# A windowed-attention kernel on one core: smaller first loads, v masked by ScalarE in the first strip, a wait moved in the loop, and fifteen matmuls ahead of the first strip

## Chip, cores and metric

One NeuronCore of a Trainium2 chip runs the kernel in one launch. The metric is the device time in microseconds (us); it is the median of three runs. All data are float32.

## What is computed

The input is an image batch of 4 x 128 channels x 96 x 96. It is normalised by groups, goes through ReLU linear attention in windows of 4 x 4 pixels, once on the projected pixels and once on their 5 x 5 average pools, then through a projection with batch normalisation, and is added to the input.

```python
def _gn(v, G=32, eps=1e-05):
    ...
    return ((g - m) / jnp.sqrt(s + eps)).reshape(v.shape)      # over 4 channels and all pixels

def _L0_conv_ref(x, qkv_w, proj_w, bn_gamma, bn_beta, bn_mean, bn_var):
    # x is cut into windows of 4 x 4 pixels
    qkv = jnp.einsum('nchw,oc->nohw', xw, qkv_w)
    pooled = _avg_pool5(qkv)
    msq = jnp.concatenate([qkv, pooled], axis=1)               # 16 heads of each, 8 numbers
    q, k = relu(msq[..., :8]), relu(msq[..., 8:16])
    v = jnp.pad(msq[..., 16:], ..., constant_values=1.0)       # a ninth column of ones
    kv = jnp.einsum('ngld,nglm->ngdm', k, v)
    out = jnp.einsum('ngld,ngdm->nglm', q, kv)
    out = out[..., :-1] / (out[..., -1:] + 1e-15)
    ...
    y = jnp.einsum('nchw,oc->nohw', out, proj_w)
    return y * inv[None, :, None, None] + (bn_beta - bn_mean * inv)[None, :, None, None]

x = x + _L0_conv_ref(_gn(x), ...)
```

## The kernel before

The 96 rows of each of the four images are cut into strips of four rows: 24 strips of an image, 96 in all, each with 384 pixels (24 windows) in the free dimension and the channels on the partitions. All of x stays on chip, in `x_all`. The order of work is written out by hand for each engine; semaphores tie the engines together, each with a count that goes up by one a strip.

**Head.** SyncE (SP) issues six loads of four strips each (L216) and then the constants and weights (L219), which raise `loaded_w`. VectorE takes the statistics of each strip as its load lands (L453), forms the group mean and variance (L461 to L488, with one square root by ScalarE, L407), normalises strip 0 (L517, signal `xn_ready`) and pools it (L509, signal `xp_ready`). GpSimd does the same for strip 1 (L286, L292, L264) and for all later strips.

**One strip.** TensorE multiplies the normalised strip by the weights of k and v (`conv_kv`, L659: three matmuls; `conv_kv_pooled`, L668: two). ScalarE writes k with ReLU (`relu_k`, L344, signal `km_f`) and copies v (`copy_v`, L355, signal `v_copied`). The windows of a tile must be kept apart in the product of k and v. For the full part this is done by four DMAs (`spread_v`, L234, signal `vm_f`) that copy every fourth row of `v_full` into its own copy in `vm_full`, which is zero elsewhere; for the pooled part by six ScalarE passes with a scale of 0 or a weight per partition (`masked_v_pooled`, L366, signal `vm_p`), between the second and the third of which `copy_y_pooled` (L403, signal `y_copied`) copies the pooled result of the strip before. `kv_products` and `kv_products_pooled` (L687) form k·v, VectorE masks it by heads (`own_heads`, L561, signals `kvc_f`, `kvc_p`), `out_products` and `out_products_pooled` (L703) multiply with q, VectorE divides (L592 to L596), TensorE transposes (L778) and projects (`project`, L787 and L789, signals `y_f`, `y_p`). VectorE adds the full part to x (L567, signal `added_f`), GpSimd the pooled part (`residual_pooled`, L264), and SP stores the strip.

**Order on TensorE.** Each pass through `step` handles the convolution of strip s + 1, transposes and projection of strip s - 1, output products of strip s, and the products of k and v of strip s + 1. Steps 1 to 94 are a loop of two steps a round. A PSUM bank serves several purposes, which is what some of the waits are for: banks 2 and 3 take the convolution and later the pooled output products, banks 0 and 1 the projection and later the products of k and v. Ahead of the pooled output products stands a wait for `added_f` and `y_copied` with a no-op (L756 to L758).

**Between the head and the loop** the batch normalisation is folded into the projection: VectorE computes its factors after ScalarE's second square root and scales `proj_sb` (L629 to L637, signal `proj_scaled`), TensorE transposes it (L811), VectorE copies it out (L644, signal `projT_ready`) and fills the ones columns of `vm_pool` (L641, signal `ones_set`).

## Time and profile before

| | |
|---|---|
| runs | 887.57, 884.42, 886.83 us; median 886.83 |
| profiled execution | 886.18 us, of which its span 884.3 us |
| TensorE (PE) busy | 848.4 us, 96% of the span |
| VectorE (DVE) busy | 699.9 us, 79% |
| GpSimd (POOL) busy | 658.9 us, 75% |
| ScalarE (ACT) busy | 480.9 us, 54% |
| DMA, mean over the span | 68 GB/s |

The span runs from the first instruction to the last. The profile gives times in microseconds from its start. PE is the stream of matmuls, PEld the loading of their weights, SPq the DMA queue's issues. One float32 matmul shows as two records. "Idle before" is the time that an engine stood still ahead of a row, and what released it; "issue" means that the profile shows nothing that it waited for.

### The profile page before, as it was taken

The numbers are of one execution on the slowest core, as the hardware profiler recorded it, in microseconds if no ns is written. First come the engines' busy times: TensorE is split into PE (matmuls) and PEld (weight loads), VectorE is DVE, ScalarE is ACT, GpSimd is POOL, SyncE is SP. The second block draws the span as 40 slices with busy tenths as digits, with TensorE's granted clock in tenths as the row PEclk, the third lists the DMA queues.
The fourth block names the chain that finished last, engine by engine and source line by source line (L and its number), as shares of the span: only waits on it lengthen the run. The fifth ranks groups of instructions, "written<-read, shape, count | busy, mean of one in ns | idle before, by whom it ended". The sixth has DMA issues, their size and how long they took to land.

```text
span 884.3 us, 63772 instructions
## 1 busy us (share of the span) xinstructions
PE 848.4 (96%) x28322; PEld 693.0 (78%) x28322; DVE 699.9 (79%) x1252; ACT 480.9 (54%) x1349; POOL 658.9 (75%) x1624
## 2 busy tenths in 40 slices
PE   0789999999999999999999999999999999999997
PEld 0568888888888888888888888888888888888885
DVE  7758888887778888888777888888777777777776
ACT  0346565646465655555555556565656564646563
POOL 2558787878787878777878777787878787878781
PEclk9999999999999999999999999999999999999999
DMA  6122322111123323111113232211111111111111
GB/s 236 40 77 81 103 84 82 49 47 48 47 69 97 91 94 98 51 48 47 49 50 99 86 98 88 82 51 48 48 50 46 49 48 47 48 47 48 47 49 47
DMA packets 39081, 60.06 MB, mean 68 GB/s; under 512 B 8560, under 2 KB 33648, under 8 KB 39024
## 3 DMA queue, kind: packets, MB, share of 16 engines
q1 hardware_dynamic: 39024, 59.52, 20.0%
q14 instruction: 48, 0.39, 0.1%
q8 instruction: 9, 0.15, 0.1%
HBM read 19.38 MB, written 18.87 MB: 43 GB/s over the span
## 4 chain that ended last, share of the span: by engine, by line
PE 94%; DVE 3%; issue 1%; DMA 1%; SPq 0%; ACT 0%; DVEq 0%
PE ps L703 24%; PE ps L687 17%; PE ps L659 14%; PE ps L668 9%; PE ps L675 9%; PE ps L787 7%; PE ps L778 6%; PE ps L789 4%; PE ps L676 4%; DVE stats L453 1%; DMA x_all<-x 0%; DVE kvc_full L561 0%; DVE kvc_pool L561 0%; DMA vm_full<-v_full 0%; DVE kvc_full L509 0%
## 5 line engine op out<-in xcount | busy, mean ns | idle before, releaser
L366 ACT ACTIVATE vm_pool<-ps,cst 128x256 f32<-128x256 f32 x576 | 230.1, 480 | 0.0
L376 ACT ACTIVATE q_full<-ps 128x384 f32<-128x384 f32 x96 | 47.2, 491 | 281.0 <-PE ps L675 281.0
L561 DVE TENSOR_TENSOR kvc_full<-ps,cst 128x864 f32<-128x864 f32 x192 | 193.2, 1048 | 4.7 <-PE ps L687 4.7
L561 DVE TENSOR_TENSOR kvc_pool<-ps,cst 128x864 f32<-128x864 f32 x192 | 193.2, 1048 | 0.5 <-PE ps L687 0.5
L286 POOL TENSOR_TENSOR xd<-x_all,mean_t 128x384 f32<-128x384 f32 x95 | 78.6, 827 | 154.3 <-PE ps L676 137.8
L659 PE MATMUL ps<-wkv_sb,xn 128*128 128x256 f32 x576 | 141.4, 382 | 23.1 <-DVE xn L517 23.1
L264 POOL TENSOR_TENSOR x_all<-y_pool,x_all 128x96 f32<-128x96 f32 x380 | 148.9, 424 | 12.7 <-DVE x_all L567 7.2
L659 PEld LDWEIGHTS ps<-wkv_sb,xn 128*128 128x128 f32 x576 | 109.4, 191 | 33.2 <-issue 23.0
L703 PEld LDWEIGHTS ps<-kvc_full,q_full 64*32 64x32 f32 x9216 | 108.3, 105 | 26.0 <-issue 26.0
L292 POOL TENSOR_TENSOR xn<-xd,rstd_t 128x96 f32<-128x96 f32 x380 | 121.8, 367 | 8.1 <-DVE xn L517 0.7
L703 PE MATMUL ps<-kvc_full,q_full 64*32 64x72 f32 x9216 | 125.0, 230 | 0.6 <-DVE kvc_pool L561 0.6
L703 PE MATMUL ps<-kvc_pool,q_pool 64*32 64x72 f32 x9216 | 116.1, 231 | 2.3 <-issue 2.2
L567 DVE SCALAR_TENSOR_TENSOR x_all<-ps,shift,x_all 128x384 f32<-128x384 f32 x96 | 59.3, 618 | 62.3 <-PE ps L787 57.7
L703 PEld LDWEIGHTS ps<-kvc_pool,q_pool 64*32 64x32 f32 x9216 | 101.8, 105 | 3.1 <-issue 3.0
L668 PE MATMUL ps<-wkv_sb,xp 128*128 128x256 f32 x384 | 99.7, 382 | 0.7 <-ACT q_pool L384 0.6
L687 PE MATMUL ps<-vm_full,k_full 64*32 64x144 f32 x4608 | 95.4, 288 | 2.3 <-issue 1.5
L687 PE MATMUL ps<-vm_pool,k_pool 64*32 64x216 f32 x3072 | 94.9, 345 | 1.9 <-issue 1.9
L264 POOL TENSOR_TENSOR hs<-ht,xn 128x96 f32<-128x96 f32 x190 | 84.0, 442 | 14.9
L355 ACT ACTIVATE v_full<-ps 128x384 f32<-128x384 f32 x96 | 47.3, 492 | 86.1 <-PE ps L659 86.0
L592 DVE TENSOR_SCALAR den_full<-ps 128x48 f32<-128x48 f32 x96 | 20.0, 208 | 90.1 <-PE ps L703 89.7
L675 PE MATMUL ps<-xn,wq_sb 128*128 128x384 f32 x192 | 87.6, 538 | 0.0
L787 PE MATMUL ps<-o_sb,projT 128*128 128x384 f32 x192 | 78.5, 491 | 0.0
(74 smaller groups left out, 1316.2 us busy)
## 6 DMA issues: line engine op xcount, KB each, us to landing
vm_full<-v_full SPq DMA_DIRECT2D x384, 54.0 KB, 1.9
out<-x_all SPq DMA_DIRECT2D x96, 192.0 KB, 1.9
x_all<-x SPq DMA_DIRECT2D x36, 384.0 KB, 3.4
x_all<-x SPq DMA_DIRECT2D x6, 768.0 KB, 7.9
cst<-consts SPq DMA_DIRECT2D x1, 170.0 KB, 11.0
wkv_sb<-wkv SPq DMA_DIRECT2D x1, 128.0 KB, 10.8
o_sb<-proj SPq DMA_DIRECT2D x1, 128.0 KB, 10.1
wq_sb<-wq SPq DMA_DIRECT2D x1, 64.0 KB, 10.6
```

The lines of the kernel that those rows point to most:

```text
L264: return pool.tensor_tensor(o, a, b, ALU.add)
L286: link(pool.tensor_tensor(xd[:], x_all[:, s * SP:(s + 1) * SP], mean, ALU.subtract), 1)
L292: last = pool.tensor_tensor(xr[:, r], rows[:, r], rstd, ALU.mult)
L366: last = act.activation(heads[:, e, :, :, 0:D], src, ACT.Copy, scale=col(C_VP + e))
L561: last = dve.tensor_tensor(kvc[:, g], src.to_broadcast(shape), own, ALU.mult)
L567: dve.scalar_tensor_tensor(xs, ps[:, Y_F, 0:SP], shift[:], xs, ALU.add, ALU.add).then_inc(added_f, 1)
L659: last = pe.matmul(ps[:, bank, at:at + 2 * P], xn[:, p, t * P:(t + 1) * P], wkv_sb[:], start=True, stop=True)
L668: last = pe.matmul(ps[:, KV_P, t * 2 * P:(t + 1) * 2 * P], xp[:, p, t * P:(t + 1) * P], wkv_sb[:], start=True, stop=True)
L675: pe.matmul(ps[:, Q_F, 0:SP], wq_sb[:], xn[:, p], start=True, stop=True).then_inc(q_f, 1)
L687: last = pe.matmul(ps[Q4 * i:Q4 * (i + 1), bank + r, t * n:(t + 1) * n], k[rows, t, Q4 * i:Q4 * (i + 1)], vm[rows, :, t, i * KC:(i + 1) * KC],
L703: last = pe.matmul(ps[Q4 * c:Q4 * (c + 1), bank + g, t * n:(t + 1) * n], blocks[rows, 4 * t + c, Q4 * e:Q4 * (e + 1)], kvc[rows, r, w], st ...
L787: pe.matmul(ps[:, Y_F, 0:SP], projT[:, 0:P], o_sb[:, 0:SP], start=True, stop=True).then_inc(y_f, 1)
```

## The change

1. The first image is loaded in nine pieces of 1, 1, 2, 4, 4, 4, 4, 2 and 2 strips in place of six of four.
2. `vm_full` of strip 0 is no longer filled by a copy and four DMAs but by four ScalarE passes straight from PSUM with a scale of 0 or 1 per partition (`masked_v_first`, signal `vm_first`); the constants have four new columns for it. The second square root stands after these passes.
3. GpSimd writes the ones columns of both masked copies once the weights are there; VectorE wrote those of `vm_pool` before.
4. TensorE turns the projection after `kv_products(0)`, in another bank, in place of ahead of the convolution of strip 1.
5. TensorE runs fifteen matmuls of 256 columns on ones before its first real matmul, as soon as weights and memsets are done.
6. In the loop the wait ahead of the pooled output products is gone. A wait for `km_f` stands ahead of the pooled projection, and a wait for `y_copied` ahead of `kv_products`. On ScalarE `copy_y_pooled` comes one pass later and waits for `added_f` too.

```diff
+        pieces = [1, 1, 2] + [4] * (FOURS - 2) + [2, 2]
...
         GS = 16
+        WARM_UP = 15
...
-            for i in range(FOURS):
-                sp.dma_start(x_all[:, 4 * i * SP:4 * (i + 1) * SP],
-                             x_v[:, 0, 4 * i * SP:4 * (i + 1) * SP]).then_inc(loaded_first[i], 16)
+            at = 0
+            for i, n in enumerate(pieces):
+                sp.dma_start(x_all[:, at:at + n * SP], x_v[:, 0, at:at + n * SP]).then_inc(loaded_first[i], 16)
+                at += n * SP
...
-            spread_v(0)
...
             pool.wait_ge(pads_zero, 5)
+            pool.wait_ge(loaded_w, 16 * 5)
+            for vm, n, first_col in ((vm_full, EF, C_VF), (vm_pool, EP, C_TP)):
+                for e in range(n):
+                    ones = vm[:, e].rearrange("p t (h c) -> p t h c", c=HC)[:, :, :, D]
+                    last = pool.tensor_copy(ones, col(first_col + e).unsqueeze(2).to_broadcast(list(ones.shape)))
+            last.then_inc(ones_set, 1)
...
+            def masked_v_first():
+
+                act.wait_ge(conv_f, 1)
+                act.wait_ge(ones_set, 1)
+                heads = vm_full[:].rearrange("p e t (h c) -> p e t h c", c=HC)
+                src = kv_tiles(KV_F, TF)[:, :, P:].rearrange("p t (h m) -> p t h m", m=D)
+                for e in range(EF):
+                    last = act.activation(heads[:, e, :, :, 0:D], src, ACT.Copy, scale=col(C_VF + e))
+                last.then_inc(vm_first, 1)
...
-                    if between is not None and e == 1:
+                    if between is not None and e == 2:
                         copy_y_pooled(between)
...
             def copy_y_pooled(s):
+
                 act.wait_ge(y_p, s + 1)
+                act.wait_ge(added_f, s + 1)
...
+            pe.wait_ge(pads_zero, 5)
+            ones = v_full[:].rearrange("p t c -> p (t c)")
+            for i in range(WARM_UP):
+                pe.matmul(ps[:, KV_P, 0:2 * P], ones[:, 0:P], ones[:, 0:2 * P], start=True, stop=True)
...
-                pe.wait_ge(vm_f, 16 * EF * (s + 1))
+                if is_first(s):
+                    pe.wait_ge(vm_first, 1)
+                else:
+                    pe.wait_ge(vm_f, 16 * EF * s)
+
+                wait(pe, y_copied, s - 1)
                 pe.nop(nofuse=True)
...
-                else:
-
-                    pe.wait_ge(added_f, s)
-                    pe.wait_ge(y_copied, s)
                     pe.nop(nofuse=True)
...
                 pe.wait_ge(o_p, s + 1)
+                if out_next:
+                    pe.wait_ge(km_f, s + 3)
                 pe.matmul(ps[:, Y_P, 0:SPP], projT[:, P:2 * P], o_sb[:, SP:],
```

TensorE at the start of the program, before: the convolution of strip 0 stands first, and the projection (`cst,o_sb`) is turned ahead of the convolution of strip 1.

```order
L659 MATMUL ps<-wkv_sb,xn 128x256 [waits xn_ready,loaded_w]
L659 MATMUL ps<-wkv_sb,xn 128x256 x2
L668 MATMUL ps<-wkv_sb,xp 128x256 [waits xp_ready]
L668 MATMUL ps<-wkv_sb,xp 128x256
L811 MATMUL ps<-cst,o_sb 128x128 [waits proj_scaled]
L811 MATMUL ps<-cst,o_sb 128x128
L659 MATMUL ps<-wkv_sb,xn 128x256 [waits xn_ready,km_f,v_copied]
L659 MATMUL ps<-wkv_sb,xn 128x256 x2
L687 MATMUL ps<-vm_full,k_full 32x144 [waits vm_f,km_f,projT_ready,ones_set]
```

The same place of the changed kernel, line numbers its own:

```order
L680 MATMUL ps<-v_full 128x256 [waits pads_zero,loaded_w]
L680 MATMUL ps<-v_full 128x256 x14
L688 MATMUL ps<-wkv_sb,xn 128x256 [waits xn_ready]
L688 MATMUL ps<-wkv_sb,xn 128x256 x2
L697 MATMUL ps<-wkv_sb,xp 128x256 [waits xp_ready]
L697 MATMUL ps<-wkv_sb,xp 128x256
L688 MATMUL ps<-wkv_sb,xn 128x256 [waits xn_ready,km_f,vm_first]
L688 MATMUL ps<-wkv_sb,xn 128x256 x2
L716 MATMUL ps<-vm_full,k_full 32x144 [waits km_f,vm_first]
L716 MATMUL ps<-vm_full,k_full 32x144 x23
L847 MATMUL ps<-cst,o_sb 128x128 [waits proj_scaled]
L847 MATMUL ps<-cst,o_sb 128x128
```

Fifteen matmuls stand ahead, and the two transposes have moved behind the products of strip 0, which no longer wait for the projection.

TensorE in the loop, from the projection to the products of the next strip, before:

```order
L787 MATMUL ps<-o_sb,projT 128x384 [waits kvc_p,o_f]
L789 MATMUL ps<-o_sb,projT 128x216 [waits o_p]
L703 MATMUL ps<-kvc_full,q_full 32x72 x48
L703 MATMUL ps<-kvc_pool,q_pool 32x72 [waits added_f,y_copied]
L703 MATMUL ps<-kvc_pool,q_pool 32x72 x47
L712 REGISTER_ALU
L687 MATMUL ps<-vm_full,k_full 32x144 [waits vm_f]
```

And in the changed kernel:

```order
L816 MATMUL ps<-o_sb,projT 128x384 [waits kvc_p,o_f]
L820 MATMUL ps<-o_sb,projT 128x216 [waits km_f,o_p]
L732 MATMUL ps<-kvc_full,q_full 32x72 x48
L732 MATMUL ps<-kvc_pool,q_pool 32x72 x48
L744 REGISTER_ALU
L716 MATMUL ps<-vm_full,k_full 32x144 [waits vm_f,y_copied]
```

The wait in the middle of the 96 output products is gone, and the one for the pooled copy stands at the products of k and v.

## Rows read from the trace of the kernel before

**Rows 1.** Windows: stretch, its length, busy time by engine (instructions), TensorE's clock, DMA.
```profile
61.45:65.20 3.75, 3.75 (x118) 2.86 (x119) 2.39 (x5) 0.00 (x0) 0.00 (x0) 0.54 0.16 58
78.78:87.53 8.75, 8.75 (x296) 7.18 (x295) 7.50 (x14) 4.97 (x15) 6.86 (x18) 1.00 0.31 93
...
400.00:600.00 200.00, 199.96 (x6780) 164.17 (x6778) 163.18 (x287) 114.09 (x322) 158.06 (x391) 1.00 0.22 71
```

**Rows 2.** The line that loads the first image: duration in ns, starts, landing.
```profile
L216 SPq DMA_DIRECT2D x_all<-x x6: 386/438/715, 0.7 to 3.4; - x6
...
DMA to landing us min/median/max: 4.4/7.9/11.2
```

**Rows 3.** Timeline of the head: start, length, engine, line, operation, idle time before.
```profile
5.20 11.29 DVE L453 BATCH_NORM_STATS2 stats<-x_all 128x6 f32<-128x384 f32 x24 [4.31 <-DMA x_all<-x]
...
5.87 0.48 SPq L219 DMA_DIRECT2D o_sb<-proj  x1
...
21.45 0.90 POOL L286 TENSOR_TENSOR xd<-x_all,mean_t 128x384 f32<-128x384 f32 x1 [16.46 <-DVE rstd_t L488]
...
23.08 2.90 PE L659 MATMUL ps<-wkv_sb,xn 128*128 128x256 f32 x6 [23.08 <-DVE xn L517]
...
26.13 1.83 PE L668 MATMUL ps<-wkv_sb,xp 128*128 128x256 f32 x4 [0.15 <-DVE xp L509]
26.29 0.20 ACT L407 ACTIVATE std<-var 128x1 f32<-128x1 f32 x1 [5.96 <-DVE var L629]
...
26.91 0.35 POOL L264 TENSOR_TENSOR vt<-hs 128x72 f32<-128x72 f32 x1
...
28.28 2.29 ACT L366 ACTIVATE vm_pool<-ps,cst 128x256 f32<-128x256 f32 x6
...
28.33 0.44 PE L811 MATMUL ps<-cst,o_sb 128*128 128x128 f32 x2 [0.37 <-DVE o_sb L637]
...
28.88 0.41 DVE L644 COPY projT<-ps 128x256 f32<-128x256 f32 x1
...
30.85 0.98 PE L687 MATMUL ps<-vm_full,k_full 64*32 64x144 f32 x48 [0.78 <-DMA vm_full<-v_full]
...
31.91 2.02 DVE L561 TENSOR_TENSOR kvc_full<-ps,cst 128x864 f32<-128x864 f32 x2 [2.63 <-PE ps L687]
```

**Rows 4.** The page's DMA issues: KB each, us from issue to landing.
```profile
o_sb<-proj SPq DMA_DIRECT2D x1, 128.0 KB, 10.1
```

**Rows 5.** The chain of waits in order of time: a convolution at full clock.
```profile
43.05 1.29 PE ps L659 x6
```

**Rows 6.** Timeline of TensorE around its last stall in new code.
```profile
61.45 0.79 PE L703 MATMUL ps<-kvc_pool,q_pool 64*32 64x72 f32 x37 [2.19 <-issue]
...
65.06 0.93 PE L675 MATMUL ps<-xn,wq_sb 128*128 128x384 f32 x2
```

**Rows 7.** Timeline of a strip in the loop, all engines.
```profile
76.97 2.38 SPq L234 DMA_DIRECT2D vm_full<-v_full  x4
...
77.44 0.51 ACT L344 ACTIVATE k_full<-ps 128x384 f32<-128x384 f32 x1
...
78.32 0.53 PE L789 MATMUL ps<-o_sb,projT 128*128 128x216 f32 x2
...
78.78 1.29 PE L703 MATMUL ps<-kvc_full,q_full 64*32 64x72 f32 x96
78.88 0.35 ACT L403 ACTIVATE y_pool<-ps 128x216 f32<-128x216 f32 x1
...
79.85 1.20 PE L703 MATMUL ps<-kvc_pool,q_pool 64*32 64x72 f32 x96
...
80.97 0.98 PE L687 MATMUL ps<-vm_full,k_full 64*32 64x144 f32 x48
```

**Rows 8.** The line that normalises strip 0: duration in ns, least, median and most.
```profile
L517 DVE TENSOR_SCALAR xn<-x_all,mean_t,rstd_t x4: 359/373/882, 21.3 to 22.6; 128x96 f32<-128x96 f32 x4
```

**Rows 9.** The page's costliest groups: busy us, mean ns, idle us before.
```profile
L703 PE MATMUL ps<-kvc_pool,q_pool 64*32 64x72 f32 x9216 | 116.1, 231 | 2.3 <-issue 2.2
```

More of the change, by code:

```diff
@@ L37 @@
 C_TP = C_VP + EP
-C_PACK = C_TP + EP
+C_VF = C_TP + EP
+C_PACK = C_VF + EF
 N_CONST = C_PACK + P
@@ L57, in constants @@
     c[:, C_TP:C_TP + EP] = own_p * times
+    c[:, C_VF:C_VF + EF] = p[:, None] % EF == np.arange(EF)[None]
     pads = p % Q4 >= WP * PXP
@@ L149, in build @@
         loaded_w = sem("loaded_w")
-        loaded_first = [sem(f"loaded_first{i}") for i in range(FOURS)]
+        pieces = [1, 1, 2] + [4] * (FOURS - 2) + [2, 2]
+        assert sum(pieces) == SPB
+        loaded_first = [sem(f"loaded_first{i}") for i in range(len(pieces))]
         loaded_later = sem("loaded_later")
@@ L158, in build @@
         ones_set = sem("ones_set")
+        vm_first = sem("vm_first")
         mv_zero = sem("mv_zero")
@@ L227, in spread_v @@
             def spread_v(s):
-                sp.wait_ge(v_copied, s + 1)
+                sp.wait_ge(v_copied, s)
                 wait(sp, kv_f, s)
@@ L353, in copy_v @@
                 act.wait_ge(conv_f, s + 1)
-                wait(act, vm_f, 16 * EF * s)
+                wait(act, vm_f, 16 * EF * (s - 1))
                 act.activation(v_full[:].rearrange("p t (h c) -> p t h c", c=HC)[:, :, :, 0:D],
@@ L409, in _ @@
             square_root(0)
-            square_root(1)
             act.wait_ge(loaded_w, 16 * 5)
@@ L430, in step @@
                     square_root(b + 1)
-            copy_v(0)
+            masked_v_first()
             relu_k(0)
+            square_root(1)
             relu_k_pooled(0)
@@ L532, in _ @@
             dve.wait_ge(mv_zero, 1)
-            for i in range(FOURS):
+            at = 0
+            for i, n in enumerate(pieces):
                 dve.wait_ge(loaded_first[i], 16)
-                for at in range(4 * i, 4 * i + 4):
+                for at in range(at, at + n):
                     last = gather_strip(0, at)
-                last.then_inc(gathered, 1)
+                    if at % 4 == 3:
+                        last.then_inc(gathered, 1)
+                at += 1
             dve.wait_ge(gathered, FOURS)
@@ L637, in _ @@
             dve.tensor_scalar(proj_sb, proj_sb, bn_inv[:], None, ALU.mult).then_inc(proj_scaled, 1)
-            for e in range(EP):
-                ones = vm_pool[:, e].rearrange("p t (h c) -> p t h c", c=HC)[:, :, :, D]
-                last = dve.tensor_copy(ones, col(C_TP + e).unsqueeze(2).to_broadcast(list(ones.shape)))
-            last.then_inc(ones_set, 1)
             dve.wait_ge(proj_turned, 1)
-            dve.tensor_copy(projT[:], ps[:, TRF, 0:2 * P]).then_inc(projT_ready, 1)
+            dve.tensor_copy(projT[:], ps[:, Q_F, 0:2 * P]).then_inc(projT_ready, 1)
             over_strips(step)
@@ L746, in out_products_pooled @@
             def out_products_pooled(s):
-                if is_first(s):
-                    pe.wait_ge(km_f, s + 2)
-                    pe.nop(nofuse=True)
-                elif is_last(s):
-                    pe.wait_ge(kvc_p, s + 1)
-                    pe.nop(nofuse=True)
-                else:
-                    pe.wait_ge(added_f, s)
-                    pe.wait_ge(y_copied, s)
+                if is_first(s) or is_last(s):
+                    if is_first(s):
+                        pe.wait_ge(km_f, s + 2)
+                    else:
+                        pe.wait_ge(kvc_p, s + 1)
                     pe.nop(nofuse=True)
@@ L807, in _ @@
             conv_kv_pooled(0, 0)
+            pe.wait_ge(vm_first, 1)
+            pe.wait_ge(km_f, 1)
+            conv_kv(1, 1)
+            kv_products(0)
             pe.wait_ge(proj_scaled, 1)
             for z in range(2):
-                last = pe.transpose(ps[:, TRF, z * P:(z + 1) * P], proj_sb[:, z * P:(z + 1) * P], col(C_IDENT, P))
+                last = pe.transpose(ps[:, Q_F, z * P:(z + 1) * P], proj_sb[:, z * P:(z + 1) * P], col(C_IDENT, P))
             last.then_inc(proj_turned, 1)
-            pe.wait_ge(v_copied, 1)
-            pe.wait_ge(km_f, 1)
-            conv_kv(1, 1)
+            kv_products_pooled(0)
             pe.wait_ge(projT_ready, 1)
-            pe.wait_ge(ones_set, 1)
-            kv_products(0)
-            kv_products_pooled(0)
             conv_q(0, 0)
```

## The prediction

> **What bounds the kernel now.** I read the busy time by stretch first. From 200 us to the end the matmul engine is busy all the time at the full 2.4 GHz: 199.96 of 200 us in [rows 1]. The reader is to see there that in the loop nothing but TensorE's own instructions counts; VectorE, ScalarE and GpSimd have room. So an edit pays in two places only: before TensorE is saturated (the head, 0 to some 66 us) and in what TensorE itself issues in each of the 94 looped strips. A strip takes 8.75 us: the second window of [rows 1] runs from one start of a group of matmuls, 78.78, to its next, 87.53.
>
> The head I read as a timeline. Six pieces of four strips each are loaded; the first lands 4.4 us after its issue at 0.7, the last 11.2 us after its issue at 3.4, that is at 5.1 and 14.6 [rows 2], or 0.475 us of transfer per strip. VectorE's 24 statistics fill 5.20 to 16.49, 0.47 us each. So the loads and VectorE run at the same pace, and the chain from there (group mean and variance, first normalised strip) gives TensorE its first matmul at 23.08. Between 23.08 and 28.3 matmuls take about twice their later time. Then a ring follows: v is copied, four transfers spread it, the products start at 30.85 when these have landed, and VectorE's masking starts at 31.91 [rows 3].
>
> **The first pieces (1, 1, 2, 4, 4, 4, 4, 2, 2).** VectorE can begin earlier, but strips 5 to 8 still come as one piece, which lands at 5.1 + 4 x 0.475 = 7.0, and before the change VectorE got to strip 5 at 5.20 + 4 x 0.47 = 7.08. What was gained before that is spent waiting. Behind it each piece of four lands just as VectorE is done with the last. Strips 17 to 20 land at 14.6 - 4 x 0.475 = 12.7; eight strips from there end at 12.7 + 8 x 0.47 = 16.46, against 16.49 before. Worth 0.0 us. SP issues three loads more, some 0.44 us each [rows 2], ahead of the weights, but the weights queue behind the 14.6 us of x anyway: the last lands at 5.87 + 10.1 = 15.97 [rows 3, 4]. Bounds: 0.5 better (only the first strips' lead) to 0.5 worse (smaller pieces landing more slowly).
>
> **Fifteen matmuls on ones.** They wait for the weights (taken 16.1) and the memsets, and stand ahead of the first real matmul. At full clock a pair of passes over 256 columns takes 1.29 / 3 = 0.43 us [rows 5], at half clock 0.86. Two stretches show when the clock rose: after the pause before 61.45 TensorE is granted 0.54 of its clock until some 3.6 us later, 65.06 [rows 1, 6]; from 23.08 its matmuls are slow to between 27 and 28.3, 4 to 5.2 us [rows 3]. I take 4: 4.6 matmuls cold, 10.4 warm: 4.0 + 4.5 = 8.5, end at 24.6. Ends: 3.6 gives 24.4; 5.2 gives 25.3; a clock that is up at once 22.6 (then xn at 23.0 decides); one that never rises 29.0. So the ones last longer than the wait that they fill, by 1.6 us, and the first product then takes 1.3 instead of 2.6 to 2.9 [rows 3]: it ends at 24.6 + 1.3 = 25.9, just as before. The gain of the clock is paid for by the overshoot. The pooled product no longer waits for it: xp is there at 26.13, and 1.83 us become 0.9.
>
> **v masked by ScalarE.** Removed are one copy of v and the four transfers that release the products at 30.85. Added are four ScalarE passes of 128 x 384 with a scale. Not in the trace; the pooled form, 128 x 256, costs 2.29 / 6 = 0.38 [rows 3], so between 4 x 0.38 = 1.5 and, by columns, 2.3; I take 1.9. Path: product done 26.0, v masked 27.95, then k (0.5 as in [rows 7]) 28.45, second square root 28.6, product of strip 1 28.5 to 29.8, masked products 1.06 (30.85 to 31.91) to 30.85. Projection: from the end of the square root (26.29 + 0.20) to the transposes took 28.33 - 26.49 = 1.84, so 28.6 + 1.84 = 30.45, hidden by those products. The two transposes (0.44) and the copy of projT (0.41) now stand between the products and VectorE's masking: 31.7, less some 0.2 since they enter while the products drain, 31.5. Before it was 31.91. The pooled v (2.29 from 28.7) is ready at 31.0, under it. So the head gains 0.4 on the path that starts the loop. With the ones ended at 23.0 it would be some 1.6 us more, 2.0 in all.
>
> **GpSimd writes the ones columns.** Ten small copies after the weights, each no dearer than GpSimd's vt row, 0.35 for more columns [rows 3], so at most 3.5 us, done by 19.7, before 21.45 where GpSimd starts. They run beside VectorE's chain. One of its four equal operations on xn took 882 ns instead of 373 [rows 8], and GpSimd's xd ran just then [rows 3]. If all the copies fell on VectorE, xn would come up to 3.5 us later; xn has 1.6 us of cover under the ones, so cost 0, ceiling 1.9. The Trainium skill (SBUF — State Buffer, two separate sides) says that the two engines' shared port is an exclusive lock, against VectorE operations in a two-port mode or with two inputs in SBUF. By that rule only the two-input operations of that chain could be held up, each by no more than a copy, and the cost stays 0. By that rule, too, an operation that meets GpSimd's waits for all of it, which the 882 ns row bears out: it ended with xd.
>
> **The loop.** Three edits, and they are three waits moved. The wait and the no-op ahead of the pooled output products go. Equal groups of 96 passes start at 78.78, 79.85 and (the next) 80.97: 1.07 and 1.12 us, so at most 0.05 us per strip lies there, 4.7 us over 94 [rows 7]. From below: TensorE idled 2.3 us in all ahead of this group [rows 9], 2.19 of them in one stall [rows 6], so 0.1 over 95. I take 1.0 us, 0.01 a strip, nearer the idle row, since idle time is what a wait can give back. Added: the wait for k ahead of the pooled projection. k is written by 77.95, that matmul starts 78.32 [rows 7]: 0.37 of cover. Added: y_copied at the v·k products. The copy ended 79.23 and comes one pass (0.38) later, 79.6; the products start 80.97. Cover 1.35; behind it nothing of ScalarE is late, since its passes are the same ones. GpSimd reads the copy after 81. What is late next if TensorE gets faster is the fourth v transfer: issued by about 78.8, landed 1.9 later, 80.7, needed 80.97: 0.25 of cover, so the loop can give no more than that.
>
> **Sum.** 0.0 - 0.4 - 1.0 = -1.4 us. The profiled execution took 886.18 (span 884.3, some 1.9 around it) and becomes 884.8; it is 0.65 under the median of the runs, 886.83, which becomes 885.4.
>
> **Rivals.**
> The wait in the loop costs all of the 0.05. For it: the two equal groups do differ by that. Against: they differ in operands too, and the idle time is 0.1. Then -4.7 and 0.4 to 2.0 from the head: 881.7 to 880.1.
> The new wait for k bites. A sequencer that takes k's signal over 0.37 us late would put up to 0.05 us into each strip: +4.7 - 0.4, 891.1, slower. It decides where k's end plus the signal's way passes the matmul's start; elsewhere it is short: the masking at 31.91 starts 0.08 after the products' end, 30.85 + 0.98 [rows 3].
> The ones overshoot. If the clock did not rise under them, they end at 29.0, 4.4 later than assumed, and the first product is cold too (1.3): +5.7 - 1.4, 891.1. Against: both stretches rose within 5.2.
> The stalls of the instruction stream move. Three passes through new code stalled TensorE; the last, 2.19, was followed by the half clock to 65.06 [rows 1, 6], which cost 0.46 x 3.75 = 1.7 us. Sixty instructions ahead shift where they fall. If the half clock stays out, 883.7; if it comes after another too, 887.1. The runs before spread from 884.42 to 887.57, so either is ordinary.
> The change does nothing at all (the head's gain is cancelled, the loop's is 0): 886.8.
>
> **How the numbers follow.** A measurement of this kernel can tell a change of about 0.5%, 4.4 us. The forecast with its shifted stalls: 0.70. Nothing at all: 0.08. The whole 0.05 a strip, or the warm head together with absent stalls: 0.15. New wait bites: 0.04. Overshoot: 0.03. So faster 0.15, same 0.78, slower 0.07. The range takes the head from +0.5 to -2.0, the loop from 0 to -3, and the half clock's 1.7 either way: 881.5 to 888.2.
>
> **What would show it.** Statistics end at 16.4 to 16.6, and VectorE waits once before strip 5. The ones end 24.4 to 25.3, the first product takes 1.3; masking on VectorE starts about 31.5. In the loop the period goes from 8.75 to 8.74. Wrong would be: statistics done before 16; masking before 30.3; a period at or under 8.70, or over 8.77.

## The result, and the profile after

The changed kernel takes 888.5 us (median of 11 runs; the kernel before took 886.3 beside it), a ratio of 1.003 with an interval of 1.0016 to 1.0044: slower by some 2.7 us (1.4 to 3.9). The forecast was 885.4. The profiled execution of the changed kernel took 887.27 us, 1.2 under its median, its span 885.4 (before: 884.3).

First the head, as rows of the timeline (start, length, engine, line, operation, idle time before), to lie beside [rows 3] and [rows 2].

```profile
0.74 4.58 SPq L224 DMA_DIRECT2D x_all<-x  x9
...
3.35 1.02 DVE L478 BATCH_NORM_STATS2 stats<-x_all 128x6 f32<-128x384 f32 x2 [2.45 <-DMA x_all<-x]
...
6.37 1.02 DVE L478 BATCH_NORM_STATS2 stats<-x_all 128x6 f32<-128x384 f32 x2 [2.00 <-DMA x_all<-x]
...
8.63 9.43 DVE L478 BATCH_NORM_STATS2 stats<-x_all 128x6 f32<-128x384 f32 x20 [1.24 <-DMA x_all<-x]
...
17.60 9.40 PE L680 MATMUL ps<-v_full 128*128 128x256 f32 x30 [17.60 <-DMA o_sb<-proj]
17.69 0.75 POOL L341 COPY vm_full<-cst 128x48 f32<-128x48 f32 x4 [12.70 <-DMA o_sb<-proj]
...
26.84 1.46 PE L688 MATMUL ps<-wkv_sb,xn 128*128 128x256 f32 x6
...
28.48 1.99 ACT L379 ACTIVATE vm_full<-ps,cst 128x384 f32<-128x384 f32 x4 [6.58 <-PE ps L688]
...
32.41 0.99 PE L716 MATMUL ps<-vm_full,k_full 64*32 64x144 f32 x48
...
34.15 2.01 DVE L589 TENSOR_TENSOR kvc_full<-ps,cst 128x864 f32<-128x864 f32 x2
```

VectorE starts its statistics 1.85 us earlier and ends them 1.57 later, at 18.06 instead of 16.49: it waits three times for x, 1.24 us even for the first piece of four. All behind it is shifted: weights, the ones, the first product, and VectorE's masking at 34.15, which stood at 31.91 in [rows 3]. Why x comes later is read from windows of one microsecond (stretch, its length, busy time by engine, clock, DMA share, GB/s), first before, then after:

```profile
2.00:3.00 1.00, 0.00 (x0) 0.00 (x0) 0.00 (x0) 0.01 (x1) 1.00 (x2) 1.00 0.66 172
3.00:4.00 1.00, 0.00 (x0) 0.00 (x0) 0.00 (x0) 0.00 (x0) 1.00 (x2) 1.00 1.02 412
4.00:5.00 1.00, 0.00 (x0) 0.00 (x0) 0.00 (x0) 0.00 (x0) 0.99 (x2) 1.00 1.00 418
```

```profile
2.00:3.00 1.00, 0.00 (x0) 0.00 (x0) 0.00 (x0) 0.01 (x1) 1.00 (x2) 1.00 0.95 300
3.00:4.00 1.00, 0.00 (x0) 0.00 (x0) 0.65 (x2) 0.00 (x0) 1.00 (x2) 1.00 0.84 152
4.00:5.00 1.00, 0.00 (x0) 0.00 (x0) 0.37 (x1) 0.00 (x0) 0.99 (x2) 1.00 0.90 313
...
6.00:7.00 1.00, 0.00 (x0) 0.00 (x0) 0.63 (x2) 0.00 (x0) 0.00 (x0) 1.00 0.95 363
```

From 3 to 4 us the small pieces move 152 GB/s where before 412 moved, and from 6 to 7 us still 363 (before: 424). The share of time that the DMA engines were busy fell much less in that microsecond, from 1.02 to 0.84, so they mostly moved less while busy; what held them no run shows.

Now TensorE's passage through new code, beside [rows 6]. These are the rows of the changed kernel that begin with a pause, and what stands around the third and fourth:

```profile
42.74 0.59 PE L716 MATMUL ps<-vm_full,k_full 64*32 64x144 f32 x23 [1.83 <-issue]
...
52.80 0.46 PE L732 MATMUL ps<-kvc_pool,q_pool 64*32 64x72 f32 x24 [1.71 <-issue]
...
62.98 0.91 PE L732 MATMUL ps<-kvc_pool,q_pool 64*32 64x72 f32 x67 [1.75 <-issue]
63.78 1.58 PE L716 MATMUL ps<-vm_full,k_full 64*32 64x144 f32 x48
65.01 1.05 PE L716 MATMUL ps<-vm_pool,k_pool 64*32 64x216 f32 x12
66.48 1.35 PE L716 MATMUL ps<-vm_pool,k_pool 64*32 64x216 f32 x20 [0.42 <-issue]
67.76 0.91 PE L704 MATMUL ps<-xn,wq_sb 128*128 128x384 f32 x2
```

Three pauses are the ones that the kernel before has too. The fourth, 12 passes into the pooled masked product of the loop's second strip, is new. It is short here; that stretch ran at half clock (granted 0.50 from 63.98 to 67.40), and TensorE came to the place later. The four pauses add up to 5.71 us, the three of the kernel before to 5.56: in this pair of executions the delay comes from the head (VectorE's masking is 2.24 late) and not from the pauses. The product with wq that stood at 65.06 in [rows 6] stands at 67.76: 2.7 us late when the first pass through the loop is over. The loop then gives back a little. The pooled product with wq comes once a strip, in two passes. Each row gives the start of the first pass and of the last in its stretch, first before, then after:

```profile
L676 PE MATMUL ps<-xp,wq_sb x4: 346/346/346, 100.8 to 109.8; 128*128 128x216 f32 x4
...
L676 PE MATMUL ps<-xp,wq_sb x6: 346/346/346, 855.3 to 873.0; 128*128 128x216 f32 x6
```

```profile
L705 PE MATMUL ps<-xp,wq_sb x4: 346/346/346, 103.6 to 112.5; 128*128 128x216 f32 x4
...
L705 PE MATMUL ps<-xp,wq_sb x6: 346/346/346, 856.6 to 874.3; 128*128 128x216 f32 x6
```

From 100.8 to 873.0, which is 88 strips and one pass in both kernels, are 772.2 us, from 103.6 to 874.3 are 770.7. So in this pair of executions the change loses 2.8 us before 104 us and wins 1.5 back in the loop.

### The profile page after: what moved, and what is told of

Its sections match the earlier page's. It is cut to its first block, busy times and chain, and to the rows that moved or that the text cites. A ratio compares the mean times of both kernels' runs of the same rounds, so it can differ in the third digit from the quotient of the medians.

```text
span 885.4 us, 63838 instructions
## 1 busy us (share of the span) xinstructions
PE 854.4 (97%) x28352; PEld 695.2 (79%) x28352; DVE 700.9 (79%) x1246; ACT 482.8 (55%) x1352; POOL 660.0 (75%) x1634
## 4 chain that ended last, share of the span: by engine, by line
PE 96%; DVE 1%; DMA 1%; issue 1%; SPq 1%; ACT 0%; DVEq 0%; ACTq 0%
PE ps L732 24%; PE ps L716 17%; PE ps L688 14%; PE ps L697 9%; PE ps L704 9%; PE ps L816 7%; PE ps L807 6%; PE ps L820 4%; PE ps L705 4%; DMA o_sb<-proj 1%; PE ps L680 1%; SPq L224 0%; DVE kvc_full L589 0%; SPq L227 0%; ACT vm_full L379 0%
## 5 line engine op out<-in xcount | busy, mean ns | idle before, releaser
L732 PE MATMUL ps<-kvc_pool,q_pool 64*32 64x72 f32 x9216 | 120.8, 231 | 3.5 <-issue 3.5
L732 PEld LDWEIGHTS ps<-kvc_pool,q_pool 64*32 64x32 f32 x9216 | 104.0, 105 | 4.0 <-issue 4.0
L816 PE MATMUL ps<-o_sb,projT 128*128 128x384 f32 x192 | 80.6, 501 | 0.0
## 6 DMA issues: line engine op xcount, KB each, us to landing
wkv_sb<-wkv SPq DMA_DIRECT2D x1, 128.0 KB, 10.2
```

Source lines behind the costliest of these rows:

```text
L732: last = pe.matmul(ps[Q4 * c:Q4 * (c + 1), bank + g, t * n:(t + 1) * n], blocks[rows, 4 * t + c, Q4 * e:Q4 * (e + 1)], kvc[rows, r, w], st ...
L816: pe.matmul(ps[:, Y_F, 0:SP], projT[:, 0:P], o_sb[:, 0:SP], start=True, stop=True).then_inc(y_f, 1)
```

## The experiments

Theory A: the nine pieces cost the head 1.6 us, and all else is as forecast. Theory B: the ones cost, by their duration or by the clock. Theory C, formed after the first runs: the ones cost as instructions, because they push the end of the loop over one more place at which TensorE's stream of instructions is refilled. In the expectations a "record" is one entry of TensorE in the trace, of a matmul's pass, of a load of weights or of its sequencer, counted from the first; one float32 product makes four. All ratios are to the kernel before, run beside, with the 95% interval; 0.001 is 0.9 us.

### The pieces

```diff
-        pieces = [1, 1, 2] + [4] * (FOURS - 2) + [2, 2]
+        pieces = [4] * FOURS
```

> The changed kernel with the first image loaded in six pieces of four strips again; all else as changed. Theory A (the nine pieces cost the head: their start leaves DMA engines idle, and three engines stay about 1 us behind to the end): statistics end at 16.5 instead of 18.1, the weights land at 16.0 instead of 17.5, the ones start 1.5 earlier, VectorE's first masking starts at 32.6 instead of 34.15, and the time is 1.5 us under the changed kernel's. Theory B (as predicted: the pieces cost 0.0, the lateness of this profile is chance or comes from another edit): statistics still end near 18, the time is the changed kernel's within 0.5 us.

Measured 885.94, ratio 1.0005 (0.999 to 1.0021). The end of the statistics, VectorE's masking and the fourth pause in its trace:

```profile
5.47 11.27 DVE L478 BATCH_NORM_STATS2 stats<-x_all 128x6 f32<-128x384 f32 x24 [4.58 <-DMA x_all<-x]
...
31.52 2.01 DVE L589 TENSOR_TENSOR kvc_full<-ps,cst 128x864 f32<-128x864 f32 x2
...
65.50 0.92 PE L716 MATMUL ps<-vm_pool,k_pool 64*32 64x216 f32 x20 [2.75 <-issue]
```

Statistics end at 16.74 and VectorE masks at 31.52, so the head stands 0.4 earlier than before, just as the sum said. By the two ratios (1.003 and 1.0005) the pieces are worth some 2 us of the 2.7, give or take 2. But the time is not under the kernel before.

The other way round, the kernel before with the nine pieces alone:

> The kernel before with the nine pieces alone. Theory A: statistics end at 18.0 instead of 16.5, all of the head comes 1.5 us later, ratio to the kernel before 1.0017. Theory B: no difference, ratio 1.000.

887.19, ratio 1.0015 (1.0002 to 1.0027), so 1.3 us (0.2 to 2.4); the statistics end at 18.28 and VectorE masks at 33.65, 1.74 later than before. Its timeline up to 17.4 us shows the same three bursts:

```profile
3.23 1.02 DVE L456 BATCH_NORM_STATS2 stats<-x_all 128x6 f32<-128x384 f32 x2 [2.33 <-DMA x_all<-x]
6.76 1.02 DVE L456 BATCH_NORM_STATS2 stats<-x_all 128x6 f32<-128x384 f32 x2 [2.51 <-DMA x_all<-x]
8.63 9.19 DVE L456 BATCH_NORM_STATS2 stats<-x_all 128x6 f32<-128x384 f32 x19 [0.85 <-DMA x_all<-x]
```

Whether it is the small pieces at the start or those at the end was asked with pieces of 4, 4, 4, 4, 4, 2, 2 and ten ones:

> As the run with six pieces and ten ones, but the last piece cut in two of two strips each, seven in all. If small pieces cost only where the engines have nothing queued (the start), statistics end at 16.5 to 16.8 as with six and the time is that run's; if every cut costs, they end 0.3 us later or more. The cut at the end can gain nothing by the prediction's sum, since strips 17 to 20 set the end.

885.48, ratio 1.0000 (0.9983 to 1.0017). Statistics run without a gap, 5.48 to 16.69. The two halves at the end cost the statistics nothing; by subtraction the cost is that of 1, 1, 2 at the start.

### The waits of the loop

The kernel before with the waits of the loop alone (the wait ahead of the pooled output products taken out, those for `km_f` and `y_copied` in their new places, `copy_y_pooled` one pass later):

> The kernel before with the moved waits of the loop alone (and the pooled copy one pass later). Predicted: 0.01 us a strip, 1.0 us in all, ratio 0.999, period 8.76 instead of 8.77. Rival: all of the 0.05 that two equal groups differ by, 4.7 us, ratio 0.995. Rival: nothing, since TensorE's backlog hides the wait, ratio 1.000; then the difference between the two profiles in the loop is something else.

884.89, ratio 0.9990 (0.9978 to 1.0003), which is not clear of no change, and 100.9 to 871.8, 770.9 us, for the stretch that took 772.2. Over all profiles of this study the period between those products is 8.771 us on average in eight kernels with the old waits (8.764 to 8.777) and 8.761 in twelve with the new (8.747 to 8.770). The groups overlap a little; the averages differ by 0.010 a strip, 0.9 us in all.

### The ones: left out, alone, fewer

```diff
-        WARM_UP = 15
+        WARM_UP = 0
```

> The changed kernel without the fifteen matmuls on ones. Theory A (the ones overshoot by 2.2 us, and give back 1.3 us on the first product and 0.8 on the pooled one): the first product starts at 24.7 instead of 26.8 and ends at 27.6 instead of 28.3, cold; VectorE's first masking about 0.7 us earlier, the time 0.5 to 1 us under the changed kernel's. Theory B (the warm clock is worth more than the overshoot because what follows is TensorE's too): the time is 0.5 to 1.5 us over the changed kernel's.

888.76, ratio 1.0032 (1.0018 to 1.0046): as slow as with the ones. The first product takes 2.90 again, but VectorE masks earlier than in the changed kernel, at 33.06. A new pause of 2.36 us stands in the output products of strip 0, ahead of 40.92, where the kernel before has none. Fifteen ones put into the kernel before:

> The kernel before with the fifteen matmuls on ones alone. Stated by the six-piece run of the changed kernel: ones from 16.2 to 24.2, so the first product starts 1.1 us late and ends 25.6 instead of 25.98, warm. ScalarE's copy waits for the second square root (26.3) all the same, so the products of k and v start at 30.8 as before. Theory A (only the head counts): ratio 1.000 within 0.001. Theory C (sixty more instructions ahead shift the blocks of the instruction stream against the work, and stalls in new code get longer or more): the head is as before, but the sum of TensorE's idle times between 35 and 70 us grows by over 1 us and the ratio is 1.001 to 1.003.

887.52, ratio 1.0026 (1.0012 to 1.0040), though VectorE masks at 32.10, hardly later than before. A fourth pause shows at the end of the loop's code:

```profile
61.23 0.91 PE L709 MATMUL ps<-kvc_pool,q_pool 64*32 64x72 f32 x67 [1.30 <-issue]
62.02 0.98 PE L693 MATMUL ps<-vm_full,k_full 64*32 64x144 f32 x48
62.76 0.58 PE L693 MATMUL ps<-vm_pool,k_pool 64*32 64x216 f32 x11
65.55 0.92 PE L693 MATMUL ps<-vm_pool,k_pool 64*32 64x216 f32 x21 [2.21 <-issue]
```

Masking by ScalarE alone (six pieces, no ones, old waits in the loop):

> The kernel before with v of the first strip masked by ScalarE, the ones columns written by GpSimd, the square root and the transposes of the projection moved, and nothing else of the change: six pieces, no ones, the waits of the loop as before. Theory A: v masked from 26.0, products of k and v about 30.0, VectorE's first masking 31.6 instead of 31.9, ratio 0.9995 to 1.000. Theory C: as in the run without ones, a stall of over 2 us at the first output products that the kernel before has not (its first fetch of instructions started at 32.6, there only at 38.5); ratio 1.001 to 1.003.

888.90, ratio 1.0036 (1.0023 to 1.0048), the slowest. VectorE masks at 33.64, 1.7 later than before: the clock rose late, and the product of strip 1 took 2.9 too. And the pause ahead of record 449 is there again (2.34). Ten ones instead of fifteen, with six pieces:

> The changed kernel with six pieces and ten matmuls on ones in place of fifteen. Theory A (overshoot): the ones end at about 22.1, before the first strip comes at 23.1, the first product ends at 24.4, the products of k and v start at 28.7 and VectorE's first masking at 30.4, 1.1 before the six-piece run with fifteen; the time is 0.5 to 1.5 us under that run's 885.9. Theory C: the head comes earlier by as much, the time does not, since the stalls grow.

887.45, ratio 1.0023 (1.0001 to 1.0045). The head is the best so far (first product 23.20, VectorE masks at 30.62, 1.3 earlier than before), and the kernel is no faster. Its pauses are 2.35, 2.23 and 1.16, and a fourth of 2.23 at record 1985. So the length of the head alone doesn't explain the time; theory B in its plain form falls. The kernel with ten ones and seven pieces differs from this one in the last piece alone and has nearly the same pauses (7.92 us in sum, here 7.97), yet its ratio was 1.0000. The intervals of the two overlap; a single ratio can't settle 2 us.

### Instructions without work

Theory C was put to the test by putting instructions ahead of the kernel before that do next to nothing, where TensorE waits anyway. First no-ops, 32 and 12:

> The kernel before with 32 instructions that do nothing ahead of TensorE's first wait, where it waits until 16 us anyway. Theory of the instruction stream: TensorE stalled at its records 705, 1217 and 1729 in the kernel before, and its loop's body ends (branch at record 1959) 26 records ahead of the next such place, 1985; with 32 more the body ends behind it. So a fourth stall of 2.2 to 2.75 us at record 1985, near 64 us, seldom made up behind it, as in the three kernels with 40 or 60 more records ahead: +1.5 us, 887.5, ratio 1.0015 to 1.0025. Rival, that the ones cost by what they compute or by the clock: nothing is multiplied here, so 886.0, ratio 1.000, three stalls.

> The same with 12 such instructions: the loop's branch stands near record 1971, still ahead of 1985. Theory of the place: three stalls as before, 886.0, ratio 1.000 within 0.0007. Rival, that any instructions ahead cost in proportion: 12/32 of what 32 cost, some 0.6 us.

886.72, ratio 1.0000 (0.9984 to 1.0015), and 887.04, ratio 1.0005 (0.9993 to 1.0018), pauses in both at records 705, 1217 and 1729 as before. The expectation for 32 (1.0015 to 1.0025) was missed. This does not speak against the theory: no record of them is in the trace and no pause moved by 32 or 12, so they are not in the stream as it ran. They are two more runs of the old kernel, with 1.0000 and 1.0005. The second try was with small products:

```diff
+            pe.wait_ge(pads_zero, 5)
+            ones = v_full[:].rearrange("p t c -> p (t c)")
+            for i in range(8):
+                pe.matmul(ps[:, KV_P, 0:4], ones[:, 0:P], ones[:, 0:4], start=True, stop=True)
```

> The kernel before with eight products of 4 columns (32 records, some 0.3 us in all) on TensorE at 16 us, where it waits for the first strip anyway. The 32 instructions that do nothing, tried earlier, had left every stall at the same record, so they can't have stood in the stream; these stand in it. Theory of the stream: the loop's branch moves from record 1959 to 1991, behind 1985, so a fourth stall of 2.2 to 2.75 us near 64 us, and 887.2 to 888, ratio 1.001 to 1.002 (15 ones alone gave 1.0026). Rival, that ones cost by their duration, by the clock or by what they read: these cost nothing, three stalls, ratio 1.000.

888.95 (before 887.24 beside it), ratio 1.0021 (1.0006 to 1.0037), where the theory said 1.001 to 1.002. Eight products over four columns, done at 19.6 and followed by more than 3 us of waiting, cost 1.9 us (0.5 to 3.3), though VectorE masks at 31.83, no later than before. Averaged, the fifteen ones alone and these give 1.0024, the two kernels with no-ops 1.0002, each within some 0.001 (an estimate from the four intervals). The timeline of TensorE at their start and at the end of the loop's code:

```profile
16.05 3.58 PE L656 MATMUL ps<-v_full 128*128 128x4 f32 x16 [16.05 <-DMA o_sb<-proj]
...
61.68 0.98 PE L692 MATMUL ps<-vm_full,k_full 64*32 64x144 f32 x48
62.41 0.94 PE L692 MATMUL ps<-vm_pool,k_pool 64*32 64x216 f32 x25
65.33 0.57 PE L692 MATMUL ps<-vm_pool,k_pool 64*32 64x216 f32 x7 [1.98 <-issue]
```

The pause has moved with the count. With fifteen ones (30 passes and 30 loads of weights, 60 records) it stood behind pass 11 of the pooled masked product; with eight tiny products (32 records) it stands behind pass 25. Fourteen passes and fourteen loads are 28 records, just what stands less ahead. That the places are fixed in the stream is seen too in windows from pause to pause of this kernel (passes and weight loads are the first two counts):

```profile
40.93:51.52 10.59, 8.29 (x252) 6.67 (x252) 5.79 (x8) 4.98 (x14) 6.86 (x17) 1.00 0.21 62
51.52:60.99 9.47, 8.51 (x252) 6.83 (x252) 6.66 (x11) 4.98 (x14) 5.65 (x14) 1.00 0.14 48
60.99:65.32 4.33, 2.35 (x126) 1.90 (x127) 2.90 (x5) 0.00 (x0) 1.23 (x4) 1.00 0.48 140
```

252 + 252, and with the sequencer's own records 512, 512, and then 256. The kernel before has the same 512 between its three pauses, but its loop branches back before the next 256 are through:

```profile
40.87:50.82 9.95, 8.46 (x252) 6.68 (x251) 5.28 (x10) 4.98 (x14) 6.84 (x17) 1.00 0.22 66
50.82:61.43 10.61, 8.43 (x253) 6.80 (x253) 5.79 (x8) 4.98 (x14) 6.84 (x17) 1.00 0.26 80
```

Three such products, 12 records:

> The same with three such products, 12 records: the branch stands near 1971, ahead of 1985. Theory of the place: three stalls at 705, 1217 and 1729, none at 1985, ratio 1.000. Rival, a cost in proportion to the records ahead: 12/32 of what eight cost.

887.40, ratio 1.0007 (0.9989 to 1.0025). The time can't be told from no change, nor from the rival's 12/32 of 1.9, 0.7 us; the expectation on the place was wrong. There is a pause of 0.98 ahead of the very last pass of the loop's body:

```profile
67.08 0.34 PE L681 MATMUL ps<-xp,wq_sb 128*128 128x216 f32 x1 [0.98 <-issue]
```

That is 20 records further on than with eight products, again as the count asks: the 7 passes that were left of the pooled masked product, the 2 of the product with wq and the first of its pooled form are ten passes. So the place was right and the room was not: the branch's own record had been counted, in order of time, and the room ahead of the place is some ten records, not 26.

### In search of a version that keeps the head's gain

If instructions cost and not time, the clock should be raised by few and long ones. Ones in a short hardware loop (three times two products of 400 columns), in the changed kernel with six pieces, and in the kernel before with the new waits:

> The changed kernel with the six first pieces of before and with its ones multiplied in a loop: three times round two products of 400 columns, some 8 products records and a branch in place of 60 records. Theory of the stream: the loop of strips ends ahead of record 1985, so no fourth stall; the head gains as with ten ones (VectorE's masking near 30.6 where before 31.9), the later waits of the loop give 1.1 more: 883.5 to 884.5, ratio 0.997 to 0.9985. Rival, that the ones disturb otherwise: as with ten ones in a row, 887.4. Rival, that the short loop's own branches stall TensorE: ones end behind 24.6 us and the head is no earlier than with fifteen ones, 885.9.

> The kernel before with the changed waits of the loop alone and the ones in the same short loop; masked v by DMA as before. Theory of the stream: three stalls as with the waits alone (884.9); the warm products of the first strip end 1.1 us earlier, but the way by the copy of v and its DMAs to VectorE's masking gives only 0 to 0.8 of it: 884.0 to 885.0, ratio 0.998 to 0.999. Rival, that ones cost whatever their count of instructions: 886.4, as ones alone cost 1.5.

888.06, ratio 1.0015 (0.9999 to 1.0030), and 887.51, ratio 1.0007 (0.9995 to 1.0020). Neither as hoped. The loop has instructions of its own, and the body of the strips' loop ends just at the place again (pauses of 1.27 and 0.84 there). The first has the pause at 449 besides (2.39), though VectorE masks at 30.82. Its profile has 10.2 us at half clock from 37.5 on. In the second the full clock brings nothing: its first product ends at 24.85, but ScalarE's copy of v starts only at 26.71, behind the second square root (26.60), which waits for VectorE; the DMAs of v follow, and VectorE masks at 32.22.

Four products of 512 columns, issued when the statistics are combined, and four tiny ones, both with six pieces and the rest of the change:

```diff
+            pe.wait_ge(dv_group, 1)
+            for i in range(4):
+                pe.matmul(ps[:, KV_P, :], x_all[:, 0:P], x_all[:, 0:512], start=True, stop=True)
```

> The changed kernel with six first pieces, and in place of the fifteen ones four products of 512 columns of x (16 records, 4.9 us) that start when the statistics are combined, at 17.7, and end at 22.6, ahead of the first strip at 23.2. Theory of the stream: the branch stands at 1982, just ahead of 1985: no fourth stall; the first products take 1.5 us, VectorE masks near 30.6: 883.5 to 884.5, ratio 0.997 to 0.9985, if the fetch at record 193 starts as with the ones. Rival: masking by ScalarE without sixty records ahead loses the fetch at 193 whatever stands there, as in the two kernels without ones: a stall of 2.4 us at record 449, 887 to 889, ratio 1.001 to 1.003.

> The same with four products of 4 columns, 16 records and 0.2 us: first products at half clock (2.9 us). If the stall at record 449 follows from the count of records ahead, it is here as in the run with four wide products or in neither; if from the time at which TensorE comes to record 193, the two differ. With it 887.5 to 889; without it VectorE masks near 31.8 and the time is 884.5 to 885.5.

> The kernel with four wide products once more, the same program: if the stall at record 449 follows from the program (where TensorE stands when it comes to 193), it is in this profile too, 2.4 to 2.6 us; if it is a matter of the execution, it can be gone, with the next stall at 705 near 2.2 in place of 0.6. The time again within 0.0018 of 0.9998, or lower if the earlier runs had the stall by chance.

Wide: 886.36, ratio 0.9998 (0.9980 to 1.0016), and once more 887.44, ratio 1.0022 (1.0009 to 1.0036); together about 1.001. Tiny: 888.70, ratio 1.0016 (0.9997 to 1.0035); VectorE masks at 33.57 and not near 31.8, since the products of strip 1 too ran at half clock (2.90). The same program of four wide products measured twice differs by 0.0024: so far can a ratio wander. The wide one has the best head of all (VectorE masks at 30.43) and loses it at record 449:

```profile
23.01 1.56 PE L688 MATMUL ps<-wkv_sb,xn 128*128 128x256 f32 x6 [0.39 <-DVE xn L542]
...
34.52 1.20 PE L732 MATMUL ps<-kvc_full,q_full 64*32 64x72 f32 x96 [0.64 <-DVE kvc_pool L589]
35.51 0.35 PE L732 MATMUL ps<-kvc_pool,q_pool 64*32 64x72 f32 x10
38.48 1.54 PE L732 MATMUL ps<-kvc_pool,q_pool 64*32 64x72 f32 x83 [2.62 <-issue]
```

The repeated program has it at the same pass (2.62 too), and the tiny one, with the same records at other times, has not. So this pause doesn't follow from the count alone, and it was no accident of one execution. Nor does the time at which TensorE comes to record 193 decide it, as the expectation supposed: 30.30 and 30.54 in the two profiles with wide products, where the pause stands, but 30.27 with ten ones, where it is missing. The queue that fetches instructions tells what is missing. In the kernel before its first fetch of a block starts at 32.6, behind record 193 (32.0); with four wide products none is there until TensorE has come to record 449 (35.64; the fetch starts at 36.0). The last try used two wide products, 8 records:

> The changed kernel with six first pieces, and in place of the ones two products of 512 columns (8 records, 2.45 us) from 20.5 to 22.95, right ahead of the first strip. Theory of the stream: 12 records ahead brought the loop's last products to the edge of record 1985 (a stall of 1.0 to 1.3 us), 8 leave them ahead of it: no stall there. The clock is granted in full during the first strip's products and not ahead of them: they take 1.5 to 2.9 us, VectorE masks near 31.2: 884 to 885.5, ratio 0.997 to 0.999, if the fetch at 193 comes; with a stall at 449, 886.5 to 887. Rival, that v masked by ScalarE costs by itself (without ones VectorE masked at 33.6, 1.7 us later than before): masking near 33, 887.5 to 889.

888.22, ratio 1.0030 (1.0019 to 1.0042). The place at 1985 has no pause, as said, and VectorE masks at 31.38; but the pause at 449 is there, 2.56, and the one behind it is 1.46. No kernel of the study is measurably faster than the one before; the nearest is the one with the loop's waits alone.

## Why the prediction was wrong, step by step

**The pieces (0.0, bounds 0.5 either way): this step failed.** It was 1.57 us in the trace, and 1.3 (nine pieces alone) and 2.2 (the changed kernel against six pieces) in time. The forecast let every piece flow at the 0.475 us per strip of the large ones. The chain "strips 5 to 8 land at 7.0" is where it broke: the piece with them landed at 8.6. The bound "smaller pieces landing more slowly" was named, and was taken from no row; a small transfer was in the trace nowhere.

**The ones (end at 24.6).** They started at 17.60 instead of 16.1, because the weights queue behind x, and they took 9.4 us, not 8.5. The first 5.4 us went at half clock (13 of the 30 passes, 0.43 from one to the next, behind them 0.22), against 2.9 us in the kernel with six pieces. The forecast had taken 4 us at half clock, out of 3.6 to 5.2. So the ones end at 27.0 and not at 24.6, and VectorE masks 2.6 later than with six pieces: 1.4 from the later weights, 1.2 from the longer half clock. That the gain is paid for by the overshoot was right; so was 1.3 for the first product (1.46), and GpSimd's columns at 0: they took 1.65 us, done at 19.3, and VectorE's chain from the end of the statistics to the end of L513 (before: L488) is 4.81 us in both kernels. In the two rows the column of the granted clock says 1.00 throughout, since the profile has no entry of it before 23.0; the half clock is read from the passes.

```profile
17.60:23.00 5.40, 5.40 (x13) 4.32 (x14) 4.54 (x19) 0.20 (x1) 1.68 (x11) 1.00 0.00 0
23.00:27.00 4.00, 4.00 (x20) 3.53 (x19) 3.83 (x10) 0.00 (x0) 2.95 (x6) 1.00 0.00 0
```

**v masked by ScalarE (-0.4).** The four passes took 1.99 against 1.9, and with six pieces VectorE masks at 31.52 against the 31.5 of the forecast. This term held in the head, to 0.02 us, and came to nothing in the time. It depends on the clock: in the kernel with the masking alone both first products ran at half clock, and VectorE masked 1.7 later than before.

**The stalls of the instruction stream, put at nothing in the sum: the second step that failed.** The rival was right in kind and too small. It said that sixty instructions ahead shift where the stalls fall, and priced only the half clock behind one of them (883.7 or 887.1). What was left out is that a shift can add a stall. The kernel's loop ended some ten records ahead of the next place; the fourth pause is there in each of the ten profiles with 12 or more records ahead in line (0.42 in the changed kernel's own, at half clock, and 0.98 to 2.75 in the others) and in none of the eight with 8 or fewer. Eight tiny products cost 1.9 us, fifteen ones alone 2.3.

How head, pauses and clock add up can be read from the 20 profiles. Take the start of the pooled product with wq that is the first behind 100 us, and subtract the start of VectorE's masking, the sum of the pauses (those of 0.2 us or more) and half of the time at half clock in between: 60.8 to 62.4 us are left, 61.9 on average, while the starts themselves spread from 100.5 to 106.5. The pauses sum to 5.0 to 6.5 us in the five kernels with neither a fourth pause nor one at record 449, and to 5.7 to 8.9 in the others.

**The loop (-1.0).** Right in the traces: -1.5 between the two profiles, -0.9 over all. The time of the kernel with the new waits alone, -0.9 (-1.9 to 0.3), agrees and isn't clear of 0. No pause came from the new wait for k. The period of 8.75 was read from a single strip; it is 8.77 on average before the change.

**The sum made again:** +1.6 for the pieces, +1.9 for the fourth stall (taken from the eight tiny products; the changed kernel's own profile has only 0.42 of it), -0.4 and -0.9 are +2.2; measured +2.7 (1.4 to 3.9). The longer half clock under the ones, 1.0 over the head of this sum in the changed kernel's profile, would make it +3.2; how many executions have it no run shows. With six pieces +0.6; measured +0.4, which the interval (-0.9 to 1.9) would also allow for much else. The range's upper end, 888.2, left out the fourth stall and held the pieces to 0.5. It was also narrower than its own terms: added up from 886.8 they give 880.1 to 889.0. And for 5.2 us at half clock the forecast's rates give an end of the ones at 25.15, not 25.3; nothing rests on it. The first sign that the prediction named did catch it: statistics were to end at 16.4 to 16.6, and ended at 18.06.

What stays open: why the fetch at record 193 is missing in six profiles of kernels with v masked by ScalarE, and not in five others. The half clock is the second thing that stays a matter of chance. Spells of 3.4 to 10.2 us at 1.2 GHz, with 1.7 to 5.1 us lost, stand in the first 71 us of 15 of these 20 profiles, and between 71 us and the last 6 in none. All 17 of them begin in a pause of TensorE or within 1.6 us behind its end. So each further pause may also be an occasion for the clock to fall; the same program of four wide products had one spell of 3.4 us in one profile and two, 10.2 together, in the other.

## What to carry to other kernels

A loop whose code fits just ahead of the next block of instructions is a resource: before adding instructions ahead of it, count where its branch falls, and look in the trace for pauses in "issue" whose distances, in records, are multiples of one number. An instruction in idle time is free only if what it displaces in the stream is. The first transfer of a load should be no smaller than one whose duration a row of the trace shows; that a consumer starts earlier is no gain if the last piece comes later.

## What the runs showed of the hardware

**Blocks of 256 instructions.** TensorE paused in new code at records 705, 1217 and 1729 in all 18 kernels that had no short loop ahead, 0.6 to 2.8 us each. Each pause belongs to a fetch: in the kernel before one starts at 38.46 and lasts 1.10; TensorE's last record ahead of the pause starts at 38.72, and it goes on at 40.88.

```profile
q8 instruction: 1, 0.02, 5.8%
```

That row is the queue's in the stretch 38.4 to 39.6: one packet, 0.02 MB. From record 449 (37.16) to the release of record 705 are 3.7 us, and 256 records of small products pass in 1.5 to 1.6, so TensorE outruns the fetch wherever a block holds nothing but these; blocks with the convolutions and waits of a strip in them (5.1 to 6.7 us here) hide it. The Trainium skill (Runtime: NRT & Kernel Launch, Instruction fetch mechanics) says that the stream is refilled in blocks of 256 instructions and that crossing a boundary is mostly hidden. The trace agrees on the 256 (the places 449, 705, 1217, 1729 and 1985 are multiples of 256 apart), and not on the second here: the crossings of one passage through new code cost 5.0 to 8.9 us of pauses in these profiles.

**Small transfers at the start.** Two pieces of one strip and one of two, issued some 0.5 us apart, left 152 GB/s in a microsecond that before had 412, and the load of the first image ended 1.6 us later (the last landing 11.4 us after its issue at 4.8, before 11.2 after 3.4).

**Tiny products are not tiny.** Eight products of 4 columns took 3.58 us, 0.45 each, where one of 256 columns takes 0.85 at half clock and 0.43 at full. The expectation was 0.3 us in all.

**The clock.** The half-clock passes under the fifteen ones lasted 5.4 us in the changed kernel, 2.9 with six pieces and 4.0 in the kernel before with the ones alone; under ten ones 3.7 and 5.8. From these rows what a warm-up buys can't be forecast closer than that.
